# Value matmuls with tokens on partitions, and the softmax sums dividing their output, in the last two layers of a one-core kernel

## The reference, cut to what matters

```
for l in range(2):
    q, k, v = split(shift_token(x) @ wqkv[l])        # 8 heads of 64
    q = l2norm(q) * q_scale;  k = l2norm(k) * k_scale
    q, k = rotary_xpos(q, k)
    sim  = q k^T * 8     # 64 queries against their own and the previous 64 keys, masked
    attn = softmax(sim)
    o    = attn @ v
    x    = x + o @ wo
    x    = x + gated_mlp(layernorm(shift_token(x)))
```

## Time and profile before

| | |
|---|---|
| median of 3 executions | 1752.42 us (1727.98 to 1760.65) |
| the profiled execution | 1759.15 us |
| its span in the trace | 1757.3 us |
| mean granted TensorE clock | 0.888 of full speed |
| both walks, from the first exponential of tile 0 to the first of tile 15 | 174.2 us and 169.0 us |

### The profile page before, as it was taken

The page is one execution under the profiler, slowest core; times in us unless marked ns, Lnnn a source line. Parts: engine busy times, 40 slices in busy tenths (PEclk is TensorE's granted clock), DMA queues, the critical chain, the costliest instruction groups (busy, mean ns, idle before and its releaser), DMA issues.

```text
span 1757.3 us, 25564 instructions
## 1 busy us (share of the span) xinstructions
PE 1452.2 (83%) x9075; PEld 839.2 (48%) x9075; DVE 1103.2 (63%) x2293; ACT 756.7 (43%) x1648; POOL 429.5 (24%) x258
## 2 busy tenths in 40 slices
PE   6999999999999599953399999972877767777766
PEld 4777777777777332330023333331555543455542
DVE  6766766766765646776356666408676635677644
ACT  2444544544543132320056655652566532555531
POOL 2000000000000113331202030002788700788811
PEclk9999999999999699975589998985899868899968
DMA  4000000000000000013111111001000000000000
GB/s 121 1 1 1 0 0 0 0 0 0 0 0 0 0 0 0 0 66 109 59 40 66 65 62 60 31 6 49 1 0 0 1 1 1 1 0 0 1 1 24
DMA packets 26097, 33.82 MB, mean 19 GB/s; under 512 B 5970, under 2 KB 20508, under 8 KB 24732
## 3 DMA queue, kind: packets, MB, share of 16 engines
q1 hardware_dynamic: 26028, 32.91, 5.9%
HBM read 28.51 MB, written 4.39 MB: 19 GB/s over the span
## 4 chain that ended last, share of the span: by engine, by line
PE 61%; POOL 14%; DVE 8%; issue 8%; ACT 3%; DMA 3%; SPq 2%; POOLq 0%; DVEq 0%; ACTq 0%
PE ps L657 13%; PE ps L688 7%; PE ps L699 7%; PE ps L893 5%; POOL ss L1949 5%; PE ps L913 5%; PE ps L871 4%; POOL probsT L1960 4%; PE ps L822 2%; POOL q_st L1947 2%; PE ps L816 2%; PE ps L644 2%; POOL k_st L1947 2%; PE ps L809 2%; POOL q_st L1953 1%
## 5 line engine op out<-in xcount | busy, mean ns | idle before, releaser
L1728 ACT ACTIVATE probsT<-ps 128x512 f32<-128x512 f32 (+1 forms) x304 | 166.2, 575 | 152.4 <-PE ps L897 137.3
L1220 DVE TENSOR_REDUCE negmax<-ps 128x1 f32<-128x1024 f32 x128 | 150.8, 1220 | 76.1 <-PE ps L688 76.1
L1628 ACT ACTIVATE probs<-ps,negmax 128x1024 f32<-128x1024 f32 x128 | 142.8, 1115 | 75.8 <-DVE negmax L1220 75.6
L1634 ACT COPY probsT<-ps 128x512 f32<-128x512 f32 x128 | 75.0, 586 | 177.7 <-PE ps L699 177.6
L1388 DVE CUSTOM_DVE_ANT_0 xn<-ps,arena 128x128 f32<-128x128 f32 (+7 forms) x128 | 93.3, 756 | 80.2 <-PE ps L871 78.8
L893 PE MATMUL ps<-arena 79*128 79x512 bf16 (+3 forms) x384 | 116.4, 348 | 32.5 <-DMA arena<-c_maxima 25.2
L699 PEld LDWEIGHTS ps<-ident,probs 128*128 128x128 f32 x1024 | 114.7, 141 | 58.4 <-issue 53.5
L699 PE MATMUL ps<-ident,probs 128*128 128x128 f32 x1024 | 136.2, 276 | 0.0
L1796 ACT ACTIVATE probsT<-ps,d_nm 128x128 f32<-128x128 f32 x256 | 90.1, 378 | 104.7 <-DVE d_nm L1520 104.7
L657 PE MATMUL ps<-probsT,v_nat 128*128 128x256 f32 x554 | 129.9, 380 | 0.0
L688 PE MATMUL ps<-k_st,q_st 64*128 64x512 f32 x512 | 127.2, 615 | 2.2 <-DVE v_st L1199 1.4
(11 more groups left out here) (255 smaller groups left out, 2853.0 us busy)
## 6 DMA issues: line engine op xcount, KB each, us to landing
arena<-c_parts SPq DMA_DIRECT2D x32, 192.0 KB
c_parts<-probsT SPq DMA_DIRECT2D x4, 768.0 KB, 4.4
yT<-c_parts SPq DMA_DIRECT2D x32, 96.0 KB
arena<-c_parts SPq DMA_DIRECT2D x16, 128.0 KB
arena<-in_L_ffn_w_dram SPq DMA_DIRECT2D x3, 512.0 KB
work<-in_L_ffn_wqkv_dram SPq DMA_DIRECT2D x1, 1536.0 KB
q_st<-c_parts SPq DMA_DIRECT2D x16, 96.0 KB
k_st<-c_parts SPq DMA_DIRECT2D x16, 96.0 KB
```

The costliest lines, as they stand in the source:

```text
L1220: dve.tensor_reduce(negmax[:, u:u + 1], s2, AX_X, ALU.max, negate=True)\
L1628: act.activation(probs[:, u % NPB, :], s2, ACT.Exp, bias=negmax[:, u:u + 1], accum_out=rowsum[:, u:u + 1]).then_inc(s_a_exp, 1)
L1728: act.activation(c_p[:, kt % 2, j0:j0 + heads, q0 - kt * P:q0 - kt * P + n], ps[:, 4 + c % 2, 0:heads * n].rearrange("p (h n) -> p h n", n ...
```

## The change

The value matmuls swap their operands: the transposed weights become stationary and v moving. Bank 2 then holds tokens on partitions and channels along the row. The weights are no longer normalised; PE transposes the raw exponentials (waiting for `s_d_e` in place of `s_d_p`). DVE multiplies the value output by the reciprocals while it brings it from PSUM to `d_on` in SBUF, as the last operation of step t for tile t-1, behind the reciprocals of tile t. PE transposes `d_on` back with four transposes at the start of the next step, between the transposes of q and k and the projection of q and k, into the same bank. ACT copies that to `d_o`, now ahead of the squares instead of behind the exponentials. POOL has only the unit norm left. The semaphore `s_fp` of the start of the program is merged into `s_w0p`, with the same order of waits.

```
 PE, step(t):   (after the transposes of q and k)
+    if exists(t, -2):
+        pe.wait_ge(s_d_on, n - 1)
+        for m in range(4):
+            ins = pe.transpose(ps[:, 2, m * P:(m + 1) * P], d_on[:, m * P:(m + 1) * P], ident[:, :])
+        ins.then_inc(s_d_ot, 1)
     if exists(t, 2):
         proj_qk(t + 2, par)
...
-    pe.wait_ge(s_d_p, n)
+    pe.wait_ge(s_d_e, n)
     (transposes of the weights of tile t-1)
...
-    ins = pe.matmul(ps[:, 3, 0:P], l_o[:, m, :], d_o[:, par, m, :],
+    ins = pe.matmul(ps[:, 3, 0:P], l_o[:, m, :], d_o[:, m, :],
...
-    ins = pe.matmul(ps[r:r + HD2, 2, m * P + i * WIN:m * P + (i + 1) * WIN],
-                    v[:, 1 - par, h * HD2:(h + 1) * HD2],
-                    d_pT[:, 4 * (h % 2) + m, i * WIN:(i + 1) * WIN], start=True, stop=True,
+    ins = pe.matmul(ps[i * WIN:(i + 1) * WIN, 2, h * HD2:(h + 1) * HD2],
+                    d_pT[:, 4 * (h % 2) + m, i * WIN:(i + 1) * WIN],
+                    v[:, 1 - par, h * HD2:(h + 1) * HD2], start=True, stop=True,
 DVE, step(t):   (last, behind the reciprocals of tile t)
+    if exists(t, -1):
+        dve.wait_ge(s_d_o, n)
+        dve.wait_ge(s_d_rr, n)
+        if exists(t, -2):
+            dve.wait_ge(s_d_ot, n - 1)
+        dve.tensor_tensor(d_on (p m c d), ps[:, 2, :] (p m c d),
+                          d_rr[:, 1 - par, :] broadcast over d, ALU.mult).then_inc(s_d_on, 1)
 ACT, step(t):   (behind the copies of q and k, ahead of square(t + 2))
+    if exists(t, -2):
+        act.wait_ge(s_d_ot, n - 1)
+        if exists(t, -3):
+            act.wait_ge(s_d_w, n - 2)
+        act.copy(d_o, ps[:, 2, :].rearrange("p (m c) -> p m c", m=4)).then_inc(s_d_oT, 1)
...
-    if exists(t, -1):
-        act.wait_ge(s_d_o, n)
-        act.copy(d_o[:, 1 - par, :, :], ...).then_inc(s_d_oT, 1)
 POOL, step(t):
-    if exists(t, 0):
-        v = d_p[:, par, :, :]
-        pool.wait_ge(s_d_rr, T0 + t + 1)
-        pool.tensor_tensor(v, v, d_rr[:, par, :] broadcast over a row, ALU.mult).then_inc(s_d_p, 1)
```

More of the change, by code:

```diff
@@ L283, in build @@
         d_qT = pf[:, 4096:4608].rearrange("p (m c) -> p m c", m=4)
-        d_o = pf[:, 4608:5632].rearrange("p (n m c) -> p n m c", n=2, m=4)
+        d_o = pf[:, 4608:5120].rearrange("p (m c) -> p m c", m=4)
+        d_on = pf[:, 5120:5632]
         d_va = pf[:, 5632:6656].rearrange("p (n c) -> p n c", n=2)
@@ L333, in build @@
         s_a_ozero = sem("s_a_ozero")
-        s_fp = sem("s_fp")
         s_ft = sem("s_ft")
@@ L424, in build @@
         s_d_rr = sem("s_d_rr")
-        s_d_p = sem("s_d_p")
+        s_d_on = sem("s_d_on")
+        s_d_ot = sem("s_d_ot")
         s_d_pt = sem("s_d_pt")
@@ L621, in _ @@
                         ins = pe.transpose(ps[:, 4 + g % 4, i * P:(i + 1) * P], fnat[:, 4 * g + i, :], ident[:, :])
-                ins.then_inc(s_fp, 1)
+                ins.then_inc(s_w0p, 1)
             def a_proj_q(b):
@@ L1055, in step @@
                         for h in range(H2):
-                            r, m = HD2 * (h % 2), h // 2
+                            m = h // 2
                             for i, v in enumerate((d_vs, d_va)):
-                                ins = pe.matmul(ps[r:r + HD2, 2, m * P + i * WIN:m * P + (i + 1) * WIN],
-                                                v[:, 1 - par, h * HD2:(h + 1) * HD2],
-                                                d_pT[:, 4 * (h % 2) + m, i * WIN:(i + 1) * WIN], start=True, stop=True,
+                                ins = pe.matmul(ps[i * WIN:(i + 1) * WIN, 2, h * HD2:(h + 1) * HD2],
+                                                d_pT[:, 4 * (h % 2) + m, i * WIN:(i + 1) * WIN],
+                                                v[:, 1 - par, h * HD2:(h + 1) * HD2], start=True, stop=True,
                                                 skip_group_check=True)
@@ L1169, in _ @@
             for g in range(9):
-                dve.wait_ge(s_fp, g + 1)
+                dve.wait_ge(s_w0p, g + 5)
                 src = ps[:, 4 + g % 4, :]
@@ L1535, in step @@
                         dve.reciprocal(d_rr[:, par, :], d_sum[:, par, :]).then_inc(s_d_rr, 1)
+                    if exists(t, -1):
[3 more added lines that the diff above has]
+                            dve.wait_ge(s_d_ot, n - 1)
+                        dve.tensor_tensor(d_on.rearrange("p (m c d) -> p m c d", m=4, c=2),
+                                          ps[:, 2, :].rearrange("p (m c d) -> p m c d", m=4, c=2),
+                                          d_rr[:, 1 - par, :].rearrange("p (c m) -> p m c", c=2).unsqueeze(3)
+                                          .to_broadcast([P, 4, 2, HD2]), ALU.mult).then_inc(s_d_on, 1)
                 rotate(0, 0)
@@ L1799, in step @@
                         ins.then_inc(s_d_e, 1)
-                    if exists(t, -1):
-                        act.wait_ge(s_d_o, n)
-                        act.copy(d_o[:, 1 - par, :, :], ps[:, 2, :].rearrange("p (m c) -> p m c", m=4))\
-                           .then_inc(s_d_oT, 1)
                 act.wait_ge(s_d_layer, l + 1)
@@ L1814, in _ @@
                 square(1, 1)
-                walk(act, step, TILES + 1)
+                walk(act, step, TILES + 2)
                 act.wait_ge(s_f_var, l + 1)
@@ L1956, in step @@
                 def step(t, par):
-                    if exists(t, 0):
-                        v = d_p[:, par, :, :]
-                        pool.wait_ge(s_d_rr, T0 + t + 1)
-                        pool.tensor_tensor(v, v, d_rr[:, par, :].unsqueeze(2).to_broadcast([P, H2, P]), ALU.mult)\
-                            .then_inc(s_d_p, 1)
                     if exists(t, 2):
@@ L1966, in _ @@
                 unit_norm(1, 1)
-                walk(pool, step, TILES)
+                walk(pool, step, TILES - 2)
             norm_out(3)
```

## The result

The changed kernel takes 1800.21 us (median of 4, 1796.94 to 1802.44) against 1749.57 us (median of 4) of the kernel before; the ratio is 1.033, with a 95% interval of 1.0234 to 1.0427. It is slower. Some executions fall into a slower state and the ratios leave them out, so a ratio need not be the quotient of the two medians beside it. The forecast was 1794 us (range 1757 to 1818), slower by over 2% with a chance of 0.57.

What follows compares the result with a forecast made beforehand. POOL's loop over two tiles was taken to bound the kernel. Middle steps +48, tile 13 to 15 -3 and ends -3 were summed to +42 us, 1794 us on the median, range 1757 to 1818.

Steps and rivals of the forecast that it cites:

- POOL leaves the path: In each tile POOL loses its 2.08 us pass over the weights and is no longer on the path.
- The projection falls behind the exponentials: On PE the q and k projection starts 4.4 us behind the first exponential, not 1.85; full-clock step 12.4 us.
- The clock: PE's clock falls in nearly every step, on projection and four transposes, adding 1.2 us: 13.6 us for each tile.
- The rival of 12.4 us: PE's clock stays up in most steps, 12.4 us each, 1761 us in all; chance 0.26.
- The scaling held by POOL's addition: DVE's scaling of the maxima is held until POOL's addition ends at 12.3 us, taking about 0.6 us, not 0.17.
- The middle steps: The 24 steps from tile 1 to tile 13 in both layers go from 278.5 to 326.4 us, +48.
- The steps from tile 13 to 15: Steps without a q and k projection, both layers together, go from 44.1 to 40.8 us, -3.
- The ends: From the first exponential of tile 15 to the last addition, -1.5 us in each layer, -3.
- The first steps: Steps 0 to 1 have no new wait and a POOL not yet late: no change.

Runs made afterwards that it cites:

- pass_kept: The changed kernel with POOL's pass over the weights put back and DVE's product made a plain copy of the same size: 1801.75 us, ratio 1.035.
- turn_later: The changed kernel with PE's four new transposes moved behind the v projection and ACT's copy of them behind its copies of v: 1707.7 us, ratio 0.981.
- the two doubled products: DVE's product done twice, once in the changed kernel (1831.4 us, ratio 1.052) and once in turn_later (1711.36 us, ratio 0.987).
- filler: The changed kernel with six useless matmuls of 256 columns in PE's wait ahead of the four new transposes: 1767.44 us, ratio 1.018.
- scale_on_act: turn_later with the scaling of the maxima moved from DVE to ACT, right ahead of the exponentials: 1687.35 us, ratio 0.966.

## Why the prediction was right, step by step

- **POOL leaves the path**: right. Its rows show waits of about 4.9 and 1.4 us in each step. pass_kept shows more than I had said: in this order its pass would have cost nothing on the whole to keep.
- **The projection falls behind the exponentials**: right, and it is the cause, shown by turn_later, which has the same operations and differs in the place of PE's wait and of ACT's copy behind it, and by the two doubled products. From the first exponential at 1626.97 I had the reciprocals at 2.94 (2.93), the product done at 3.85 (3.73: it starts 0.12 behind the start of the reciprocals), the projection at 4.4 (4.29 in filler; 4.70 where the four transposes run at the low clock), the full-clock step at 12.4 (12.28 in filler).
- **The clock**: right in kind, and 1.2 us were 1.33. It fell in 23 of the 24 steps, on the four transposes and the projection. I had the projection at 1.99 at full clock; it is 1.88 when PE comes to it without a break. The four transposes carry 0.46 us of the price, near the upper end of the "up to 0.5" that I gave them. By the rule of the Trainium skill that the prediction cites ("TensorE: Matmul & The Clock Gate", Part 4), a transpose doesn't count as PE being busy in the way that a matmul does. The trace agrees in so far as the clock was at 0.50 behind twelve of them, but it doesn't decide the point: PE also stood empty for 3.39 us there, and no run put transposes alone into the wait. Nor do the rows that I called for it: in the earlier trace rows the fast projection too came behind eight transposes (1589.48). What filler shows is that matmuls in this place keep the clock up. The rival of 12.4 us needed the clock to stay up.
- **The scaling held by POOL's addition**: right, 0.70 us in each step. In the changed kernel the scaling is longer than 0.17 us in 28 of its 32 tiles, and in all 28 it ends within 0.04 us of the end of a POOL addition; in the four without such an addition it takes 0.17. That this time is on the path is shown by scale_on_act. The Trainium skill, "GPSIMD Engine Reference", section 1, Specifications, says that GpSimd's SBUF access is shared with VectorE's instructions in a 2-port mode or with two SBUF inputs. The traces agree as far as they go: the scaling reads SBUF and is held, the copy of the weights from PSUM beside the same addition takes its 0.68 us. In which mode the scaling ran no row shows.
- **The middle steps**: +48 forecast, 326.6 - 278.5 = +48.1 measured. So close a match is in part luck: each side is one profiled execution, and the executions of the kernel before lie up to 33 us apart (1727.98 to 1760.65). The 13.61 us of the new step are firmer, as nearly all its steps are alike.
- **The steps from tile 13 to 15**: -3 forecast, -4.1 measured (1424.96 - 1404.93 and 1715.08 - 1695.06 against 44.1).
- **The ends**: -3 forecast, -0.8 measured: 1437.22 - 1424.96 = 12.3 against 12.7 us, the same in the second layer. In place of POOL's pass stand DVE's last product (1433.94, idle 0.80 before it for the value matmuls), its transposes, their copy and the output projection in a row, 3.3 us to the addition, with nothing left to cover them. The value matmuls start only 1.0 us earlier than before, at 7.8 in place of 8.8 us behind that exponential, as the four transposes stand ahead of the weights' (they take 1.12 us there), and the way from them to the addition is 0.6 us longer. That is the term that was mis-sized, by 2 us.
- **The first steps**: nothing forecast, +1.6 measured (11.27 and 10.91 against 10.45 and 10.14 us). The held scaling is part of it and belonged into the sum: at tile 1 of both layers it takes 0.70 us in place of 0.17, and in scale_on_act, where it is gone from DVE, these steps are 10.39 and 10.36 us against 11.28 and 10.90 in turn_later. The rest, 0.3 us a layer, is not followed up.

In all +44.8 us in the walks of the profiled executions, against +42 forecast. The rest of these two executions differs by -8.4 us ahead of the walks (first exponential at 1231.25 in place of 1239.68) and +1.2 between and behind them, in code that the change doesn't touch, so their spans differ by only 37.6 us, while the medians differ by 50.6. That the whole times came out near the forecast is for that part luck. The runs don't tell what moves that part.

## What to carry to other kernels

In a software pipeline on in-order engines, an operation costs by where it stands in its engine's program. Before adding one, list what is queued behind its wait: here a wait for the exponentials was put ahead of a projection that had run beside them, and moving it behind turned a loss of 3% into a gain of about 2%. Where the wait leaves PE without matmuls, count the low clock on the first work after it, transposes included; and when an engine is freed, look at what its operations now run beside. And when one path has been shortened, read again which one ends last: with ACT's squares early it was PE's own work.

## What the runs showed of the hardware that was not expected

- Twelve more matmul instructions in each step (2.75 us of useless work) made the changed kernel faster, from a ratio of 1.033 to 1.018: 1.33 us a step.
- In the changed kernel the low clock came so regularly that 22 of the 24 middle steps took between 13.5 and 13.8 us (the other two 12.27, at full clock, and 13.91). With 0.68 us more in the path the step grew by 0.89 and the steps spread from 13.6 to 15.1 us. What sets this rhythm is left open.
- GpSimd takes 2.91 us for the power of 128x16 numbers and 2.36 us for the sum of 128x1024. And not each of its operations holds DVE's scaling: in the kernel before, the scaling ran inside such a power 13 times, about 2 us or more after its start, and took 0.17 us every time.
